# Group 0 in the ramp by halves, A^T in two instructions and the variance in three operations, in a hypergraph block on one core

## What is computed

```
H  = (adj != 0)                    # 128x128 per graph
w  = adj[first row]                # weight of each hyperedge
D  = H w ; B = column sums of H    # inverted, 0 where they are 0
h  = relu(A x W1^T + b1)
h  = layer_norm(h, gamma, beta)    # over 512
y  = A (h W2^T) + b2
out = layer_norm_plain(x + (y + x))
```

## Time and profile before

| | |
|---|---|
| median of three executions | 289.74 us (289.73, 289.74, 290.66) |
| the profiled execution's own time | 290.7 us |
| its span in the profile | 288.9 us |
| PE busy | 277.7 us, 96% of the span |
| DVE, ACT, POOL busy | 79%, 68%, 48% |
| HBM traffic | 89 GB/s over the span |

### The profile page before, as it was taken

How to read it: one execution, slowest core, us unless ns; L and a number is a source line. 1 busy time by engine, 2 the same in 40 slices (tenths; PEclk the granted TensorE clock), 3 DMA queues, 4 the chain that set the end, 5 groups by cost and what they waited for, 6 DMA issues and landing times.

```text
span 288.9 us, 5778 instructions
## 1 busy us (share of the span) xinstructions
PE 277.7 (96%) x1814; PEld 249.0 (86%) x1814; DVE 227.9 (79%) x660; ACT 195.6 (68%) x556; POOL 138.6 (48%) x193
## 2 busy tenths in 40 slices
PE   6899999999999999999999999999999999999991
PEld 6779979898898989899898989899898989889880
DVE  1676579787979888797978888797988879596884
ACT  3288977766767876676677877676678775583614
POOL 2224463637364563636374463636365364536362
PEclk9999999999999999999999999999999999999998
DMA  7920140433513434431433533333423322120104
GB/s 218 309 79 19 40 127 16 112 113 63 173 41 122 113 94 115 122 114 54 152 70 93 140 99 109 100 104 53 136 50 91 97 88 75 36 73 2 50 25 145
DMA packets 37255, 27.70 MB, mean 96 GB/s; under 512 B 10013, under 2 KB 35305, under 8 KB 37225
## 3 DMA queue, kind: packets, MB, share of 16 engines
q1 hardware_dynamic: 37120, 27.30, 33.3%
q10 hardware_dynamic: 104, 0.04, 0.1%
HBM read 17.21 MB, written 8.42 MB: 89 GB/s over the span
## 4 chain that ended last, share of the span: by engine, by line
PE 85%; DVE 7%; issue 2%; POOL 2%; DMA 2%; ACT 1%; DVEq 0%; SPq 0%; POOLq 0%
PE bank_v L291 29%; PE bank_g L308 10%; PE bank_g L301 10%; PE bank_g L303 10%; PE bank_v L325 9%; PE bank_v L276 9%; PE bank_s L255 5%; PE bank_g L318 2%; DMA w_raw<-in_L_gnn_W_dram 2%; POOL rstd L870 1%; DVE g_sb L652 1%; DVE r_lo L661 1%; DVE pair_sb L666 1%; PE bank_g L333 1%; PE bank_g L353 1%
## 5 line engine op out<-in xcount | busy, mean ns | idle before, releaser
L886 POOL TENSOR_TENSOR xb_sb<-x_sb,b_half 128x512 f32<-128x512 f32 (+1 forms) x31 | 41.2, 1331 | 75.6 <-DVE r_lo L661 51.6
L481 ACT ACTIVATE r_sb<-bank_v,vec 128x512 f32<-128x512 f32 x64 | 44.2, 691 | 36.4 <-PE bank_v L291 35.7
L301 PE MATMUL bank_g<-w_hi,r_hi 128*128 128x258 f32 x256 | 65.5, 288 | 0.0
L303 PE MATMUL bank_g<-w_lo,r_hi 128*128 128x256 f32 x256 | 63.8, 282 | 0.0
L894 POOL TENSOR_SCALAR r_hi<-r_sb 128x512 fp32r<-128x512 f32 x64 | 47.9, 749 | 32.4 <-ACT r_sb L481 32.3
L661 DVE TENSOR_TENSOR r_lo<-r_sb,r_hi 128x512 fp32r<-128x512 f32 x64 | 44.7, 719 | 11.1 <-POOL r_hi L894 11.1
L291 PE MATMUL bank_v<-u_hi,w_hi 128*128 128x512 f32 x128 | 50.7, 396 | 0.4 <-DVE u_lo L625 0.4
L291 PE MATMUL bank_v<-u_hi,w_lo 128*128 128x512 f32 x128 | 50.8, 397 | 0.0
L291 PE MATMUL bank_v<-u_lo,w_hi 128*128 128x512 f32 x128 | 50.6, 395 | 0.0
L301 PEld LDWEIGHTS bank_g<-w_hi,r_hi 128*128 128x128 f32 x256 | 48.3, 189 | 1.4
L303 PEld LDWEIGHTS bank_g<-w_lo,r_hi 128*128 128x128 f32 x256 | 48.1, 188 | 1.2
(11 more groups left out here) (99 smaller groups left out, 449.1 us busy)
## 6 DMA issues: line engine op xcount, KB each, us to landing
x_sb<-in_x_dram SPq DMA_DIRECT2D x16, 512.0 KB, 3.8
out_dram<-z_sb SPq DMA_DIRECT2D x15, 512.0 KB, 3.2
adj_sb<-in_adj_dram SPq DMA_DIRECT2D x16, 256.0 KB, 4.0
d_row<-d_rows SPq DMA_DIRECT2D x13, 256.0 KB, 3.4
w_raw<-in_L_gnn_W_dram SPq DMA_DIRECT2D x2, 512.0 KB, 5.9
out_dram<-z_sb SPq DMA_DIRECT2D x2, 256.0 KB, 2.6
turned_h<-h_sb SPq DMA_TRANSPOSE x13, 2.4
d_rows<-dinv SPq DMA_DIRECT2D x13, 2.0 KB, 2.1
```

Of the source, the lines that this page charges most:

```text
L301: pe.matmul(bank_g[:, n, 0:W2COLS], r_hi[:, i % 2, k, graph(n)], w2_hi[:, k], start=(k == 0), stop=False)
L303: pe.matmul(bank_g[:, n, 0:DOUT], r_hi[:, i % 2, k, graph(n)], w2_lo[:, k], start=False, stop=False, skip_group_check=True)
L481: nc.scalar.activation(r_sb[:, k], bank_v[:, k % 2], ACT.Relu, bias=vec[:, k:k + 1]).then_inc(relu_ready, 1)
L886: nc.gpsimd.tensor_tensor(xb_sb[:, i % 2, part], x_sb[:, i % 3, part], b2_half[:, :].unsqueeze(1).to_broadcast([P, n, DOUT]), ALU.add).the ...
```

## The change

Four edits, all in the schedule of work that is otherwise the same:

1. **Group 0 by halves.** The adjacency of group 0 comes in two transfers of two graphs. H, its transposes, `ht_sb`, 1/B, `htb_sb`, `make_s`, 1/D, `a_sb`, `turn_a` and `at_sb` of group 0 are made for two graphs at a time, with semaphores of their own (`first_*`). W1 is turned and split by halves, in `bank_v`, between the halves of `make_s(0)`; W2 is turned by halves between the halves of `turn_a(0)`; `make_u(0)` writes to `bank_g` and starts on the first two graphs. There are 22 warm-up transposes ahead and 10 between the H transposes and `make_s(0)`. `make_v(0, 0)` starts on `u_hi`, before `u_lo` is there. `turn_h(1)` goes behind `make_v(0, 0)`; `make_s(1)` behind `make_v(0, 3)` and the first half of `make_c2`; `turn_a(1)` and `turn_h(2)` behind `make_g(0, 0)`. ACT and DVE orders follow.
2. **`make_at` in two instructions** of two graphs, one ahead of `make_var1(i, 1)` and one behind it.
3. **`make_var1` in three operations**: the two extra columns of `w2_hi` hold 1/512 and -1/512, so PE gives the mean and its negative; one operation per graph makes mean * (-mean) + mean square from them, one for both graphs adds epsilon. `sum_q` scales by 1/512. The wait for `q_summed` now stands ahead of all three.
4. **POOL**: `split_r(i + 1, 0)` (r_hi 0) goes ahead of `inverse_std2(i - 1)`, between the two powers.

```diff
-            load_adj(0)
+            for half in range(2):
+                sp.dma_start(adj_sb[:, 0, graphs(half)], adj_dram[:, graphs(half)]).then_inc(
+                    adj_in[0] if half else first_adj, 16)
...
+            def make_first_s(half):
+                pe.wait_ge(htb_ready if half else first_htb, 1)
+                pe.wait_ge(wcol_ready, 1)
+                for n in each(half):
+                    mm = pe.matmul(s_parts[:, half, n % 2], ht_sb[:, 0, n], htb_sb[:, 0, n], start=True, stop=True)
+                mm.then_inc(s_made if half else first_s, 1)
+
+            def turn_first_a(half):
+                pe.wait_ge(a_ready if half else first_a, 1)
+                for n in each(half):
+                    mm = pe.transpose(bank_s[:, half, graph(n % 2)], a_sb[:, n], ident[:, :])
+                mm.then_inc(a_turned if half else first_a_turned, 1)
+
+            def make_first_u():
+                pe.wait_ge(first_at, 1)
+                pe.wait_ge(x_in[0], 16)
+                for c in range(KD):
+                    pe.wait_ge(vec_ready if c else edges_ready, 1)
+                    for n in range(PER):
+                        if n == PER // 2:
+                            pe.wait_ge(at_ready, 1)
+                        mm = pe.matmul(bank_g[:, c, graph(n)], x_sb[:, 0, n, graph(c)], at_sb[:, 0, n],
+                                       start=True, stop=True)
+                    mm.then_inc(u_made, 1)
...
-            turn_h(0)
+            turn_first_h(0)
             pe.wait_ge(edges_in, 16)
-            pe.transpose(bank_v[:, 1, 0:N], edge_rows[:, :], ident[0:N, 0:N]).then_inc(edges_turned, 1)
-            turn_w1()
-            make_s(0)
+            pe.transpose(bank_g[:, 0, 0:N], edge_rows[:, :], ident[0:N, 0:N]).then_inc(edges_turned, 1)
+            turn_first_h(1)
+            for _ in range(KEEP_WARM):
+                pe.transpose(bank_q[:, :].bitcast(BF16)[:, graph(0)], ident_b[:, :], ident_b[:, :])
+            make_first_s(0)
+            turn_w1(0)
+            make_first_s(1)
+            turn_w1(1)
             pe.wait_ge(weights_in[0], 48)
-            pe.transpose(bank_v[:, 0, 0:3 * KH], vec_rows[:, :], ident[0:3 * KH, 0:3 * KH]).then_inc(vec_turned, 1)
-            turn_w2()
-            turn_a(0)
-            make_u(0)
+            pe.transpose(bank_g[:, 1, 0:3 * KH], vec_rows[:, :], ident[0:3 * KH, 0:3 * KH]).then_inc(vec_turned, 1)
+            turn_first_a(0)
+            turn_w2(0)
+            turn_first_a(1)
+            turn_w2(1)
+            make_first_u()
+            make_v(0, 0)
             turn_h(1)
-            pe.wait_ge(w1_ready, 1)
-            make_v(0, 0)
             make_v(0, 1)
+            make_v(0, 2)
             sum_w2()
-            make_v(0, 2)
+            make_v(0, 3)
+            make_c2([0, 1])
             make_s(1)
-            make_v(0, 3)
-            make_c2()
-            turn_a(1)
-            turn_h(2)
+            make_c2([2, 3])
 
             pe.wait_ge(w2_ready, 1)
             for i in range(G):
                 make_g(i, 0)
                 if i == 0:
+                    turn_a(1)
+                    turn_h(2)
...
+            read_first_ht(0)
             act.wait_ge(edges_turned, 1)
-            nc.scalar.activation(edge_cols[:, :], bank_v[:, 1, 0:N], ACT.Copy).then_inc(edges_ready, 1)
-            act.wait_ge(w1_turned, 1)
-            nc.scalar.activation(w1_hi[:, :, :], bank_g[:, 0:KD], ACT.Copy).then_inc(w1_hi_ready, 1)
+            nc.scalar.activation(edge_cols[:, :], bank_g[:, 0, 0:N], ACT.Copy).then_inc(edges_ready, 1)
+            read_first_ht(1)
+            act.wait_ge(first_d, 3)
+            for n in each(0):
+                ins = nc.scalar.activation(a_sb[:, n], s_parts[:, 0, n, 0:P], ACT.Copy, scale=dinv[:, 0, n:n + 1])
+            ins.then_inc(first_a, 1)
+            split_w1(0)
+            read_first_at(0)
+            read_first_at(1)
             act.wait_ge(vec_turned, 1)
-            nc.scalar.activation(vec[:, :], bank_v[:, 0, 0:3 * KH], ACT.Copy).then_inc(vec_ready, 1)
-            read_at(0)
+            nc.scalar.activation(vec[:, :], bank_g[:, 1, 0:3 * KH], ACT.Copy).then_inc(vec_ready, 1)
+            split_w1(1)
             split_u(0)
+            act.wait_ge(vec_ready, 1)
+            relu(0, 0)
             read_ht(1)
+            relu(0, 1)
             act.wait_ge(w2_scaled, 2)
             nc.scalar.activation(w2_t[:, :, :].rearrange("p k o -> p (k o)"),
                                  bank_g[:, 2:4].rearrange("p b o -> p (b o)"), ACT.Copy).then_inc(w2_t_ready, 1)
-            act.wait_ge(vec_ready, 1)
-            relu(0, 0)
+            relu(0, 2)
             make_htb(1)
-            relu(0, 1)
             act.wait_ge(w2_centred, 1)
             nc.scalar.activation(w2_hi[:, :, 0:DOUT], w2_g[:, :, :], ACT.Copy).then_inc(w2_hi_ready, 1)
-            relu(0, 2)
+            relu(0, 3)
             make_a(1)
-            relu(0, 3)
             read_at(1)
             read_ht(2)
...
-                nc.vector.tensor_scalar(stat1[:, 0, part], bank_g[:, part, SUM], 1.0 / HID, None,
-                                        ALU.mult).then_inc(stat1_step, 1)
-                dve.wait_ge(stat1_step, done * 3 + 1)
-                nc.vector.tensor_tensor(stat1[:, 1, part], stat1[:, 0, part], stat1[:, 0, part],
-                                        ALU.mult).then_inc(stat1_step, 1)
                 dve.wait_ge(q_summed, done + 1)
-                dve.wait_ge(stat1_step, done * 3 + 2)
-                nc.vector.scalar_tensor_tensor(out=stat1[:, 2, part], in0=sum_sq[:, part], scalar=1.0 / HID,
-                                               in1=stat1[:, 1, part], op0=ALU.mult,
-                                               op1=ALU.subtract).then_inc(stat1_step, 1)
-                dve.wait_ge(stat1_step, done * 3 + 3)
-                nc.vector.tensor_scalar(stat1[:, 3, part], stat1[:, 2, part], 0.0, EPS, ALU.max,
+                for n in each(half):
+                    ins = nc.vector.scalar_tensor_tensor(out=stat1[:, 0, n:n + 1], in0=bank_g[:, n, MEAN:MEAN + 1],
+                                                         scalar=bank_g[:, n, MEAN + 1:MEAN + 2],
+                                                         in1=sum_sq[:, n:n + 1], op0=ALU.mult, op1=ALU.add)
+                ins.then_inc(stat1_step, 1)
+                dve.wait_ge(stat1_step, done + 1)
+                nc.vector.tensor_scalar(stat1[:, 1, part], stat1[:, 0, part], 0.0, EPS, ALU.max,
                                         ALU.add).then_inc(var1_ready, 1)
...
+            make_first_h(0)
+            make_first_h(1)
+            make_first_htb(0)
+            make_first_htb(1)
+            make_first_d(0)
+            make_first_d(1)
+            dve.wait_ge(d_ready, 1)
+            for n in each(1):
+                ins = nc.vector.tensor_scalar(a_sb[:, n], s_parts[:, 1, n % 2, 0:P], dinv[:, 0, n:n + 1], None, ALU.mult)
+            ins.then_inc(a_ready, 1)
+            split_w1(0)
+            make_h(1)
+            split_w1(1)
+            split_u(0)
             scale_w2(range(KH // 2))
             scale_w2(range(KH // 2, KH))
-            make_h(1)
-            split_u(0)
             dve.wait_ge(w2_scaled, 2)
             nc.vector.tensor_tensor(w2_sum[:, :, :], w2_g[:, 0:2], w2_g[:, 2:4], ALU.add).then_inc(w2_added, 1)
             make_b(1)
             dve.wait_ge(w2_added, 1)
             nc.vector.tensor_tensor(w2_sum[:, 0], w2_sum[:, 0], w2_sum[:, 1], ALU.add).then_inc(w2_added, 1)
+            split_r(0, 0)
+            centre_w2()
+            split_r(0, 1)
             make_h(2)
-            centre_w2()
-            split_r(0, 0)
-            split_r(0, 1)
+            split_w2()
             make_d(1)
-            split_w2()
             split_r(0, 2)
             split_r(0, 3)
...
+                if i and i + 2 < G:
+                    make_at(i + 2, 0)
                 make_var1(i, 1)
                 if i and i + 2 < G:
-                    make_at(i + 2)
+                    make_at(i + 2, 1)
...
+                split_r(i + 1, 0)
                 if i:
                     inverse_std2(i - 1)
-                split_r(i + 1, 0)
                 split_r(i + 1, 1)
```

More of the change, by code:

```diff
@@ L15 @@
 EPS = 1e-5
-WARM_UP = 26
+WARM_UP = 22
+KEEP_WARM = 10
 TINY = 1.1754944e-38
@@ L261, in turn_a @@
                 for n in range(PER):
-                    mm = pe.transpose(turned_a[j][:, graph(n)], a_sb[:, n], ident[:, :])
+                    mm = pe.transpose(turned_a[:, graph(n)], a_sb[:, n], ident[:, :])
                 mm.then_inc(a_turned, 1)
@@ L327, in make_y, with turn_w1, turn_w2 @@
                 mm.then_inc(y_made, 1)
-            def turn_w1():
+            def turn_w1(c):
                 pe.wait_ge(weights_in[1], 16)
-                for c in range(KD):
-                    for k in range(KH):
-                        mm = pe.transpose(bank_g[:, c, graph(k)], w1_raw[:, k, graph(c)], ident[:, :])
```

(61 more changed lines are left out.)

85 lines of the change are left out of this document (36 added, 49 removed).

## The result

| | before | after |
|---|---|---|
| median | 289.74 us (289.73, 289.74, 289.74, 290.66) | 287.22 us (four executions, 287.19 to 287.23) |
| ratio of after to before | | 0.9905, 95% interval 0.9886 to 0.9924 |
| profiled execution, its span | 290.7, 288.9 | 287.23, 285.4 |

The account below looks back on a forecast made before the run. PE, busy 96% of the span, was the bound; only ramp, first pass and end could move. From 290.7 us, 0.85 + 0.3 + 0.6 gave 288.95 (low clock) and 2.35 gave 288.35 (high); forecast 288.6, range 288.0 to 289.4.

Parts of the forecast that it names:

- The floor at x's landing: Ramp: x landing at 10.3 us holds the gain at the high level to 2.5 us and little more.
- a rise between the two is likeliest: Sum: the clock rises between the low level's 288.95 us and the high level's 288.35, giving 288.6 us.
- the high case: Whole kernel with the clock at the high level from 6.3 us: gain 2.35 us, time 288.35 us.
- the clock rose about 2 us sooner: Ramp of the median execution, 0.96 us under the profiled one: `make_s(0)` would take 0.89 us less.
- Front of the ramp, order: Ramp by halves: `make_v(0, 1)` starts at 15.1 us instead of 17.03, a gain of 1.9 us.
- Given back: From `make_v(0, 0)` to `make_v(1, 0)`: ACT's serial list and DVE's queue return one microsecond of 1.9, leaving 0.85.
- First pass: First pass of the loop: shorter variances remove PE's wait on the DVE and POOL chain, 0.3 us (0 to 0.4).
- End: End of the kernel: variances with one operation less each save 0.6 us (0.3 to 0.8).
- A: Ramp: ACT and DVE make PE wait 1.0 us longer at `turn_q(0)`, 289.3 to 290 us; chance 0.18.
- B: Ramp: the clock rises only when `make_u(0)` is through, 291.9 us; chance 0.05.
- C: Ramp: no PE wait at `turn_q(0)` or behind w2_lo (0.4 + 0.5), high level, 287.6 us; chance 0.12.
- D: Loop: late `d_row` or dear `make_at` halves lengthen passes; 0.2 us a pass gives 291.2 us; chance 0.03.

Follow-up runs that it names:

- b_again: The kernel before, unchanged, profiled a second time: 289.56 us.
- a_low: The changed kernel with 12 warm-up transposes instead of 22 and without the ten ahead of `make_first_s(0)`: median 288.83 us, profiled at 288.67.
- a_turns: The changed kernel with `turn_a(1)` and `turn_h(2)` ahead of `make_g(0, 0)` on PE, as in the kernel before: 288.15 us.
- a_keep0: The changed kernel without its ten transposes ahead of `make_first_s(0)`: 287.16 to 287.44 us, median 287.19.
- a_sq_rlo: The kernel of a_squares with `r_lo(0, 2)` ahead of `w2_lo` and h(2) behind `r_lo(0, 3)` on DVE: 286.39, 286.42, 286.74 and 287.05 us.
- a_squares: The changed kernel with the first two squares of group 0 on ACT moved from behind `read_ht(2)` to behind `relu(0, 3)`: 286.61 us.
- b_keep_var: The kernel before with six transposes ahead of W1's turn (289.71 us), plus only the variance in three operations, mean columns and scaled sum: 288.66 us.

## Why the prediction was wrong

Starts in us; the column that decides is `turn_q(0)`:

| | level behind 6 us | `make_v(0, 1)` | `turn_q(0)` | to `turn_q(1)` | end* | time |
|---|---|---|---|---|---|---|
| before, trace of the prediction | low | 17.10 | 31.17 | 13.93 | 7.30 | 290.7 |
| before, b_again | high | 16.00 | 30.05 | 13.92 | 7.30 | 289.56 |
| after order, a_low | low | 15.17 | 30.33 | 13.53 | 6.69 | 288.67 |
| after | high | 13.66 | 28.82 | 13.55 | 6.69 | 287.23 |

*from the start of the last `r_lo` matmuls (L308, L320) to that of the last instruction.

**The step that failed** is a sentence on the front of the ramp: "At the high level from 6.3 on it is 2.5 and little more, because ACT's and DVE's part is as long as before and x lands at 2.3 + 8.0 = 10.3 us". The mechanism was seen, the term was mis-sized: at the high level the gain at `make_v(0, 1)` is 3.4 (17.10 to 13.66), not 2.5, and the level's share of it is 1.5 (15.17 to 13.66), not 0.6. It may be more: a_low started 0.45 us sooner. The matmuls and turns between `make_first_s(0)` and `make_first_u` lie one behind the other on PE: 3.60 us at the high level (6.14 to 9.74), 5.57 at the low one (5.69 to 11.26). ACT and DVE fit beside them, so all of PE's shortening counts; in a_turns four matmuls at the low level, 0.50 longer, made `make_v(0, 1)` 0.49 later. The floor at x's landing was there, but a microsecond lower: x landed at 2.8 + 6.5 = 9.3, ahead of 9.74. Where it landed at 9.8 (a_keep0), `make_first_u` started at 9.88. Had it been 10.3, some 0.56 more would have been lost (an estimate, no run has it).

The second fault is in what was made of it. The sum took the level half-way ("a rise between the two is likeliest") and the midpoint of two cases, 288.6, where the case with the reason behind it was one of them. With 1.5 in place of 0.6 the high case is 1.75 + 1.5 = 3.25 under 290.7, 287.45; 287.22 was measured. In my own estimate of the median, "the clock rose about 2 us sooner", the direction was right and the size not: in b_again it rose by 4.9 us, ahead of both W1's turn and `make_s(0)`, for 1.12 us.

The terms one by one:

- **Front of the ramp, order:** 1.9 forecast, 1.93 at the low level (17.10 to 15.17). That this agrees is in part luck: a_low started 0.6 us sooner than forecast (5.69 for 6.3) and took 0.7 longer from there (9.48 for 8.8). From the start of the changed kernel the order's share would be nearer 1.5, and the level's nearer 2.0 (an estimate; only their sum, 3.4, is measured).
- **`make_first_s(0)`:** 6.3 forecast, 6.14.
- **Given back:** one microsecond forecast; 3.44 at `make_v(0, 1)` is 2.35 at `turn_q(0)`, 1.09. The two parts that were named are there: `make_g(0, 0)` takes 1.91 us from its start to that of the next row instead of 1.52, 0.39 (0.4 forecast; a_sq_rlo shows its cause), and `make_g(0, 2)` to `turn_q(0)` 2.00 instead of 1.53, 0.47 (0.5 forecast; a_squares shows that ACT's serial list is its cause). The other 0.2 lies in the list between. At `make_v(1, 0)`, where the forecast stands, 2.11 are left, since `u_lo(1)` is late as well. That putting the turns back ahead would help was refuted by a_turns.
- **First pass:** 0.3 forecast (0 to 0.4), 0.43 by b_keep_var, 0.38 between the two profiles.
- **End:** 0.6 forecast, 0.61 by b_keep_var alone and by the two profiles. The first power of the last group starts 2.12 us behind `turn_q(15)` (272.05 to 274.17), in b_again 2.58 (273.64 to 276.22): 0.46 sooner, 0.45 forecast. In the second variance, where nothing holds DVE, three operations take 0.55 us from first start to last end and the four old ones took 0.82 (278.97 to 279.79 in the trace of before): both sizes were 0.1 too small (0.45 and 0.71 in the sum), the saving of 0.26 is right. In the first variance three take 0.66 and four took 1.29 (b_again), because POOL's addition held the second of the four (0.65 for 0.16); the new ones start 0.17 later behind `turn_q(15)`, which is the earlier wait for `q_summed` (at most 0.18 forecast). The last of the three ends at 274.09, as the addition of 2.40 us does (271.66 + 2.40 = 274.06), and takes 0.27 instead of 0.17. The Trainium skill, "SBUF — State Buffer", section "SBUF: two separate sides", lets a DVE instruction in a two-port mode and a GpSimd one exclude each other; the trace fits that, with 0.10 us on this operation. It costs the kernel no more than that, since POOL's power stands behind the same addition.
- **Edits 2 and 4:** forecast free, and free (229.68 and 229.72 us over 14 passes). The halves of `make_at` take 0.60 each, as estimated.

Against a before at the high level, the gain is 1.23 + 0.37 + 0.61 = 2.21 at the last instruction (283.83 to 281.64 is 2.19), and 2.33 in the profiled times. Against the trace of the prediction, 1.12 of level come on top: 3.3 at the last instruction. That the gain against the high kind comes to nearly the 2.35 that I had for the high case is an accident of two errors that cancel: the too small term, and a base that was 1 us too slow.

**Rivals.** A (ACT and DVE eat the rest) didn't happen: the 0.9 us lost in the two waits were in the sum already. B (the level stays low) didn't happen in any execution of the changed kernel; a_low, from its earlier start, shows that a low level up to about 10 us costs 1.5. C (287.6, no wait at `turn_q(0)` or behind w2_lo) names the gains that a_squares and a_sq_rlo got, but 287.22 was reached with both waits still there. D (the loop) didn't happen.
